# The last stage of a decoder: v in q's bank, the norm's root on GpSimd, copies swapped, one gelu from PSUM

## The chip, the cores and the metric

The kernel runs on one core of a Trainium2 chip. The metric is the device time in microseconds (us). Of the kernel before, 3 runs gave 2872.33 us in the median (2869.9 to 2873.28). In what follows PE is TensorE, DVE is VectorE, ACT is ScalarE, POOL is GpSimd and SP is SyncE, the queue that issues the DMAs.

## The reference

The program is a decoder of twelve stages over x of 4 batches, 256 tokens and width 128, all in float32. Only the last stage, `l3_ffn`, is touched. It is a small transformer of its own, six layers deep:

```
def ffn_layer(x, g, bln, W1, b1, W2, b2):
    mu = x.mean(-1, keepdims=True)
    var = ((x - mu) ** 2).mean(-1, keepdims=True)
    xn = (x - mu) / jnp.sqrt(var + 1e-05) * g + bln
    hg = xn @ W1 + b1
    a, gate = jnp.split(hg, 2, -1)
    return a * jax.nn.gelu(gate, approximate=False) @ W2 + b2
for i in range(DEPTH):                                    # 6
    x = attn_layer(shift_tokens(x), Wqkv[i], q_scale[i], k_scale[i], Wo[i]) + x
    x = ffn_layer(shift_tokens(x), ln_g[i], ln_b[i], W1[i], b1[i], W2[i], b2[i]) + x
```

`attn_layer` projects x to q, k and v (16 heads of 64), divides q and k by their norm in each head, scales and rotates them, and does a softmax attention of each block of 32 tokens to itself and the block before it. `shift_tokens` moves the upper half of the width by one token. The gates and ups of the feed-forward part are 341 wide.

## The kernel before

`l3_ffn` loads tables and weights, and calls `stream`, which is one software pipeline over the whole stage. A job is one layer of one batch: 6 x 4 = 24 jobs. A job has 8 pairs of heads, so 192 groups `g`, and 4 projection steps `u` (two halves of the heads by two blocks of 128 tokens), so 96 steps. Every engine walks the same list of ticks, one per group, and in each tick emits what is due there, in the order in which the code stands; constants say how many ticks a part of a job lies behind its first group. There is no scheduler: each engine runs its own list strictly in order, and semaphores hold it where data is missing.

In tick `s` each engine does this (names as in the code):

- PE: q's projection in even ticks (line 2077, into bank 0 of PSUM); k's (2086, bank 1) and v's (2091, bank 7) in odd ticks. Then the scores of group s (2101 adds the window mask, 2109), the turning of group s+1's q and k (2121, bank 3), the turning of group s-2's probabilities (2130), one part of a job's rest in bank 2, and the sums with v of group s-3 (2228, `heads`, the first half of bank 7).
- ACT: copies the heads of group s-4 out of bank 7 (signal `stored`), squares q or k, copies v out (`v_copied`), does the four exps of group s, copies the turned q and k of group s+1 (`net_qk_T`) if the group is even, and then the parts of a job's rest.
- DVE: the reciprocal of group s-1's sums (2407), the maximum of group s (2411), in some ticks the product for the last gate (2421), the two products of the rotation of q or k (2375 and 2381, signal `parted`), the copy of the turned probabilities, the copy of the turned q and k if the group is odd, the sums of squares (2447, even ticks), and the rest.
- POOL: multiplies group s-1's probabilities with the reciprocals (2337), in one tick of four the late half of a root for the head norms (8 steps, lines 1877 to 1880), scales group s+2 (2350), adds the rotation's two products (2329), in one tick of four the early half of the root (6 steps).

The rest of a job comes at fixed ticks, which repeat every 8 ticks, since a job has 8 groups. I number ticks by their remainder modulo 8. Tick 4 is OUT (2142, 32 matmuls). Tick 5 is LATE: PE shifts the tokens (2152 to 2154), DVE copies them to z, takes mean and variance (2464, 2467) and computes the inverse root with `root_of_variance`, eleven steps on a tile of 128x2, of which each waits for the one before (2393 to 2398), and the shift (2401). Tick 6 is SHIFT (2162). Tick 7 is ZT: ACT normalizes z with two ACTIVATEs (line 130) that wait for the root and stand ahead of that tick's exps, PE turns z (2171), ACT copies it out. Tick 0 is GATES: PE makes two thirds of the gates (2182), ACT adds the bias to each. Tick 1 is BOTH: PE makes the last third of the gates and of the ups (2190, 2191), ACT adds the bias to that third and does one gelu over all three (2309). Tick 2 is UPS: DVE first multiplies the last third (2421), then PE writes two thirds of the ups (2197), and DVE multiplies those (2479). Tick 3 is DOWN (2208).

ACT holds one table of functions at a time, and the program has an ACT_TABLE_LOAD ahead of the gelu and one ahead of the next exp.

Two rules set how v's matmul waits. v and `heads` lie in one bank, so v's matmul (2091) waits for `stored` of every group up to s-4, and the sums (2228) wait for `v_copied` of the last v. q's matmul waits for `parted` of the q before.

Of the kernel before, what the change touches and what calls it, by code (L numbers as in the profile page):

```python
# [16 lines left out]
I32 = mybir.dt.int32  # L17
# [8 lines left out]
QT = N // P  # L26
# [78 lines left out]
def decoder(nc, a, out):  # L105
    ctx = ExitStack()
    with ctx:
# [1690 lines left out]
        def l3_ffn():  # L1798
            sub = ExitStack()
            with sub:  # L1800
# [37 lines left out]
                made = signal("window_made", 4)  # L1838
                with nc.Block() as block:
                    @block.vector  # L1840
                    def _(dve):
                        nc.vector.tensor_copy(window16[:, :], window[:, :]).then_inc(made.sem, 1)
                        nc.vector.memset(gelu[:, :, :], 0.0).then_inc(made.sem, 1)
                        nc.vector.memset(by_batch(xnT[D // 2:D, :])[:, :, 0:1], 0.0).then_inc(made.sem, 1)
# [47 lines left out]
        def stream(p, GT, qkv_in, rows, weights, tables, heads_norm, ln, softmax, ffn):  # L1892
# [45 lines left out]
            LN_OPS = 11  # L1938
            ln_rooted, normed = signal("net_ln_rooted", LN_OPS * JOBS), signal("net_normed", 2 * JOBS)
            ln_shifted = signal("net_ln_shifted", JOBS)  # L1940
            z_turned, z_moved = signal("net_z_turned", JOBS), signal("net_z_moved", JOBS)
            gates_made, gates_moved = signal("net_gates_made", JOBS), signal("net_gates_moved", 3 * JOBS)
            both_made, gelued = signal("net_both_made", JOBS), signal("net_gelued", JOBS)
# [46 lines left out]
            def until_copied(eng, g):  # L1990

                if g >= 0:
                    e = ENG[g % 2]
                    eng.wait_ge(copied[e].sem, copied[e].at(0, g // 2 + 1))

            finished, sent = signal("net_finished", B), signal("net_sent", B, step=16)
            with ps("bank", [P, 8, BANK]) as bank, nc.Block() as block:
                qk_bank = (bank[:, 0, :], bank[:, 1, :])
                turn_bank, flip_bank = bank[:, 3, :], bank[:, 6, :]
                heads, v_bank = bank[:, 7, 0:N], bank[:, 7, :]  # L2000
# [55 lines left out]
                def _(pe):  # L2056
                    held, values_in = [], 0
# [6 lines left out]
                    for s in TICKS:  # L2064
                        u = at_tick(s, PROJ, 2, S)
                        if u is not None:
# [9 lines left out]
                            until(pe, parted, 2 * u - 1)  # L2076
                            nc.tensor.matmul(qk_bank[0], xnT[:, (QT * b + t) * P:(QT * b + t + 1) * P], w_qkv[:, half_cols(c)],  # L2077
                                             start=True, stop=True).then_inc(q_filled.sem, 1)
                        u = at_tick(s, PROJ + 1, 2, S)
                        if u is not None:  # L2080
# [12 lines left out]
                            values_in = u + 1  # L2093
# [81 lines left out]
                        if n is not None:  # L2175
# [9 lines left out]
                            held = [(gates_moved, 3 * n + 2)]  # L2185
# [28 lines left out]
                        if 0 <= g < G:  # L2214
# [8 lines left out]
                            until(pe, v_copied, values_in)  # L2223
# [9 lines left out]
                def _(act):  # L2233
# [7 lines left out]
                    for s in TICKS:  # L2241
# [37 lines left out]
                        if 0 <= g < G and g % 2 == 0:  # L2279
# [24 lines left out]
                        if n is not None:  # L2304
                            k = GT[2]
                            act.wait_ge(both_made.sem, both_made.at(0, n + 1))
                            affine("act", gelu[0:k, 2, :], spare[0:k, 0:N], 1.0, vec[0:k, 7:8]).then_inc(gates_moved.sem, 1)
                            act.wait_ge(gates_moved.sem, gates_moved.at(0, 3 * n + 3))
                            nc.scalar.activation(gelu[:, :, :], gelu[:, :, :], ACT.Gelu).then_inc(gelued.sem, 1)

                @block.gpsimd
                def _(pool):
# [19 lines left out]
                    for s in TICKS:  # L2332
# [33 lines left out]
                def _(dve):  # L2366
# [17 lines left out]
                    def root_of_variance(dve, n):  # L2384

                        lower, y, t = ln_temp[:, 0, :], ln_temp[:, 1, :], ln_temp[:, 2, :]
                        done = [LN_OPS * n]

                        def then(ins):
                            done[0] += 1  # L2390
                            ins.then_inc(ln_rooted.sem, 1)
                            dve.wait_ge(ln_rooted.sem, ln_rooted.at(0, done[0]))
                        then(nc.vector.tensor_scalar(lower, meanvar[:, 0:QT, 1], LN_EPS, -0.5, ALU.add, ALU.mult))
                        then(nc.vector.tensor_scalar(y.bitcast(I32), lower.bitcast(I32), -0.5, ROOT_MAGIC, ALU.mult, ALU.add))
                        for r in range(3):
# [235 lines left out]
```

## Time and profile before

| | us |
|---|---|
| median of 3 runs | 2872.33 |
| the profiled execution | 2870.53 |
| its span, first to last instruction | 2868.4 |
| last stage, first scores to last (L2101) | 1836.4 to 2824.8 |
| PE busy in the span | 2533.2 (88%) |
| DVE busy | 1777.3 (62%) |
| ACT busy | 1540.6 (54%) |
| POOL busy | 1363.8 (48%) |

The busy shares are over the whole span; the last stage is the 1050 us at its end. There the four engines are all busier, and the stage repeats itself every 8 ticks, so one period can be read closely and stands for the others. A row of the timeline gives the start, the length, the engine and line, and in brackets the idle time of that engine just before and what ended it. PEld is the load of weights that goes ahead of a matmul. PEclk is the clock that TensorE was granted, as a share of full speed.

### The profile page before, as it was taken

The numbers are of one execution on the slowest core, as the hardware profiler recorded it, in microseconds if no ns is written. First come the engines' busy times: TensorE is split into PE (matmuls) and PEld (weight loads), VectorE is DVE, ScalarE is ACT, GpSimd is POOL, SyncE is SP. The second block draws the span as 40 slices with busy tenths as digits, with TensorE's granted clock in tenths as the row PEclk, the third lists the DMA queues.
The fourth block names the chain that finished last, engine by engine and source line by source line (L and its number), as shares of the span: only waits on it lengthen the run. The fifth ranks groups of instructions, "written<-read, shape, count | busy, mean of one in ns | idle before, by whom it ended". The sixth has DMA issues, their size and how long they took to land. (4 is left out here: it accounts for less than half of the span.)

```text
span 2868.4 us, 57933 instructions
## 1 busy us (share of the span) xinstructions
PE 2533.2 (88%) x20585; PEld 1609.3 (56%) x20585; DVE 1777.3 (62%) x4074; ACT 1540.6 (54%) x4979; POOL 1363.8 (48%) x1981
## 2 busy tenths in 40 slices
PE   6999978988989979959289999689999999999996
PEld 3555545555645646646155555356666666666665
DVE  4556655545656755564645555677777777777773
ACT  1455534623746736623135555466667667666763
POOL 0344433401536623400004444587777777777772
PEclk8899997998989999989579999899999999999998
DMA  2000000000000010000010000200110101011000
GB/s 70 1 1 1 1 8 1 12 28 10 2 4 1 2 33 1 2 6 1 8 28 1 1 1 1 62 27 24 28 37 20 46 20 31 27 27 38 20 26 7
DMA packets 45711, 47.84 MB, mean 17 GB/s; under 512 B 11947, under 2 KB 31414, under 8 KB 45431
## 3 DMA queue, kind: packets, MB, share of 16 engines
q1 hardware_dynamic: 45430, 44.18, 5.6%
q8 instruction: 167, 2.74, 0.4%
q14 instruction: 114, 0.93, 0.1%
HBM read 31.05 MB, written 0.52 MB: 11 GB/s over the span
## 5 line engine op out<-in xcount | busy, mean ns | idle before, releaser
L1033 DVE TENSOR_REDUCE negmax<-scores 128x1 f32<-128x508 f32 (+4 forms) x512 | 212.6, 467 | 215.6 <-PE scores L918 184.4
L1013 POOL TENSOR_TENSOR l_xattn_probs<-l_xattn_probs,rowinv 128x512 f32<-128x512 f32 x128 | 130.3, 1039 | 421.1 <-DVE rowinv L1025 421.1
L2275 ACT ACTIVATE net_probs<-bank,net_negmax 128x96 f32<-128x96 f32 x768 | 251.7, 340 | 126.5 <-DVE net_negmax L2411 126.2
L1013 POOL TENSOR_TENSOR lora_probs<-lora_probs,rowinv 128x508 f32<-128x508 f32 (+1 forms) x256 | 149.5, 617 | 248.6 <-DVE rowinv L1025 248.6
L2329 POOL TENSOR_TENSOR net_rope<-net_rope,net_sin_parts 128x512 f32<-128x512 f32 x192 | 244.4, 1273 | 7.1 <-DVE net_sin_parts L2381 7.1
L2337 POOL TENSOR_TENSOR net_probs<-net_probs,net_inverse 128x384 f32<-128x384 f32 x192 | 158.7, 827 | 181.2 <-DVE net_inverse L2407 179.3
L2411 DVE TENSOR_REDUCE net_negmax<-bank 128x4 f32<-128x384 f32 x192 | 106.2, 553 | 196.0 <-PE bank L2109 195.3
L2350 POOL TENSOR_TENSOR net_rope<-net_rope,net_head_inv 128x512 f32<-128x512 f32 x192 | 201.2, 1048 | 7.5 <-POOL net_head_inv L1880 0.9
L124 DVE COPY turned<-flip 128x512 f32<-128x512 f32 (+3 forms) x280 | 163.2, 583 | 66.3 <-PE flip L945 52.3
L739 DVE TENSOR_REDUCE negmax<-scores 128x2 f32<-128x256 f32 (+2 forms) x192 | 157.8, 822 | 71.4 <-PE scores L647 42.0
L918 PE MATMUL scores<-kT,qM 64*128 64x512 f32 (+2 forms) x768 | 192.2, 577 | 6.0 <-ACT kT L122 2.5
L986 ACT ACTIVATE lora_probs<-scores,negmax 128x508 f32<-128x508 f32 (+1 forms) x256 | 117.8, 472 | 141.8 <-DVE negmax L1033 141.0
L122 ACT ACTIVATE turned<-flip 128x512 f32<-128x512 f32 (+3 forms) x280 | 143.5, 513 | 63.2 <-PE flip L661 53.1
L968 PE MATMUL heads<-turned,V 128*64 128x256 f32 (+1 forms) x1280 | 167.3, 383 | 2.0 <-ACT turned L122 1.4
L986 ACT ACTIVATE l_xattn_probs<-scores,negmax 128x512 f32<-128x512 f32 x128 | 86.9, 684 | 136.5 <-DVE negmax L1033 136.5
L2275 ACT ACTIVATION_READ_ACCUMULATOR net_probs<-bank,net_negmax 128x1 f32 x768 | 156.3, 204 | 0.0
L2121 PE MATMUL bank<-ident,net_rope 128*128 128x128 f32 x768 | 129.1, 292 | 26.5 <-POOL net_rope L2350 26.5
L2239 ACT ACTIVATE net_squares<-bank 128x512 f32<-128x512 f32 x192 | 115.2, 600 | 68.4 <-PE bank L2077 37.2
L724 POOL TENSOR_TENSOR cross_probs<-cross_probs,rowinv 128x1024 f32<-128x1024 f32 x64 | 119.8, 1893 | 66.3 <-DVE rowinv L734 66.3
L2091 PE MATMUL bank<-net_w_qkv,xnT 128*128 128x512 f32 x192 | 103.4, 620 | 40.7 <-ACT net_rope L122 40.7
L124 DVE COPY net_probs_turned<-bank 128x512 f32<-128x512 f32 x192 | 130.7, 681 | 13.4 <-PE bank L2130 13.3
L2375 DVE TENSOR_TENSOR net_rope<-bank,net_cos_table 128x512 f32<-128x512 f32 x192 | 130.9, 682 | 9.2 <-ACT net_squares L2239 9.1
(434 smaller groups left out, 6499.9 us busy)
## 6 DMA issues: line engine op xcount, KB each, us to landing
net_w_qkv<-in_L_ffn_Wqkv SPq DMA_DIRECT2D x12, 768.0 KB, 5.9
net_vals_between<-net_vals SPq DMA_DIRECT2D x48, 192.0 KB, 2.5
net_w_out<-in_L_ffn_Wo SPq DMA_DIRECT2D x6, 512.0 KB, 4.2
net_vals_between<-net_vals SPq DMA_DIRECT2D x48, 64.0 KB, 2.0
moe_w<-in_L_ffn_w13T SPq DMA_DIRECT2D x8, 256.0 KB, 2.7
net_w<-in_L_ffn_W SPq DMA_DIRECT2D x6, 341.0 KB
moe_w<-in_L_ffn_w2T SPq DMA_DIRECT2D x8, 128.0 KB, 2.3
ctx_tok<-in_ctx SPq DMA_DIRECT2D x1, 768.0 KB, 6.6
```

The costliest lines, as they stand in the source:

```text
L122: return nc.scalar.activation(dst, src, ACT.Copy, scale=scale)
L124: return nc.vector.tensor_copy(dst, src)
L739: nc.vector.tensor_reduce(negmax[:, c:c + 2], scores[:, 2 * half:2 * half + 2, 0:nk], AX.X, ALU.max, negate=True).then_inc(maxed.sem, 1)
L918: last = nc.tensor.matmul(scores[:, 2 * qt + h, 0:nk], qM[rows, 0, t * P:(t + 1) * P], kT[rows, k0:k0 + nk], start=True, stop=cross)
L968: last = nc.tensor.matmul(heads[rows, q0 * P:QT * P], V[:, v0 + j, rows], turned[:, 2 * p + h, c0:c0 + w], start=(j == 0), stop=(j == part ...
L986: last = nc.scalar.activation(pr[:, slot(g, qt, h), k0:k1], scores[:, 2 * qt + h, k0:k1], ACT.Exp, bias=negmax[:, u * tail + w:u * tail + ...
L1013: last = nc.gpsimd.tensor_tensor(own, own, rowinv[:, u * tail + w:u * tail + w + 1].to_broadcast([P, k1 - k0]), ALU.mult)
L1033: last = nc.vector.tensor_reduce(negmax[:, u * tail + w:u * tail + w + 1], scores[:, 2 * qt + h, k0:k1], AX.X, ALU.max, negate=True)
L2275: last = nc.scalar.activation(prob_blocks(g)[:, w, :], score_blocks(g)[:, w // 2, w % 2, :], ACT.Exp, bias=maxima[:, g % 4, w:w + 1], accu ...
L2329: nc.gpsimd.tensor_tensor(own, own, sin_parts[:, (2 * u + s) % 4, :], ALU.add).then_inc(added.sem, 1)
L2337: nc.gpsimd.tensor_tensor(prob_blocks(g), prob_blocks(g), part, ALU.mult).then_inc(shared.sem, 1)
L2350: nc.gpsimd.tensor_tensor(own, own, factor.to_broadcast([P, 4, 2, DH]), ALU.mult).then_inc(scaled.sem, 1)
```

## The change

Four things change, all in `stream`.

1. `v_bank` is bank 0, q's bank, instead of bank 7. v's matmul now waits for `parted` of the same step's q, and q's matmul waits for v's copy. The waits on `stored` ahead of v and on `v_copied` ahead of the sums go.
2. The norm's root leaves DVE. DVE writes variance plus epsilon and the negated mean (two steps), POOL raises the first to the power -0.5 and multiplies (two steps), one tick later. The exponents are a tile that DVE fills once.
3. Which engine copies the turned q and k is swapped: ACT now copies in even ticks, DVE in odd ticks.
4. The last third of the gates goes through the gelu straight from PSUM, with its bias; the gelu of the other two thirds follows. The DVE product of the last third waits only for the first of the two.

```
@@ -1990,14 +1990,14 @@
-                    e = ENG[g % 2]
+                    e = ENG[(g + 1) % 2]
...
-                heads, v_bank = bank[:, 7, 0:N], bank[:, 7, :]
+                heads, v_bank = bank[:, 7, 0:N], bank[:, 0, :]
@@ -2074,6 +2074,7 @@
                             until(pe, parted, 2 * u - 1)
+                            until(pe, v_copied, u)
...
-                            until(pe, stored, min(G, s - VALUES))
-                            until(pe, v_copied, u)
+                            until(pe, parted, 2 * u + 1)
...
                             until(pe, stored, g)
-                            until(pe, v_copied, values_in)
@@ -2304,9 +2302,9 @@
-                            affine("act", gelu[0:k, 2, :], spare[0:k, 0:N], 1.0, vec[0:k, 7:8]).then_inc(gates_moved.sem, 1)
-                            act.wait_ge(gates_moved.sem, gates_moved.at(0, 3 * n + 3))
-                            nc.scalar.activation(gelu[:, :, :], gelu[:, :, :], ACT.Gelu).then_inc(gelued.sem, 1)
+                            nc.scalar.activation(gelu[0:k, 2, :], spare[0:k, 0:N], ACT.Gelu, bias=vec[0:k, 7:8]).then_inc(gelued.sem, 1)
+                            act.wait_ge(gates_moved.sem, gates_moved.at(0, 2 * n + 2))
+                            nc.scalar.activation(gelu[:, 0:2, :], gelu[:, 0:2, :], ACT.Gelu).then_inc(gelued.sem, 1)
@@ -2358,6 +2356,14 @@
+                        n = at_tick(s, LATE + 1, PER, JOBS)
+                        if n is not None:
+                            pool.wait_ge(ln_ready.sem, ln_ready.at(0, 2 * n + 2))
+
+                            until(pool, normed, 2 * n)
+                            nc.gpsimd.tensor_tensor(ln_inv[:, :], ln_temp[:, 0, :], ln_temp[:, 2, :], ALU.pow).then_inc(ln_rooted.sem, 1)
+                            pool.wait_ge(ln_rooted.sem, ln_rooted.at(0, n + 1))
+                            nc.gpsimd.tensor_tensor(ln_shift[:, :], ln_temp[:, 1, :], ln_inv[:, :], ALU.mult).then_inc(ln_shifted.sem, 1)
@@ -2466,7 +2453,11 @@
-                            root_of_variance(dve, n)
+                            until(dve, ln_rooted, n)
+                            nc.vector.tensor_scalar(ln_temp[:, 0, :], meanvar[:, 0:QT, 1], LN_EPS, None, ALU.add).then_inc(ln_ready.sem, 1)
+
+                            until(dve, ln_shifted, n)
+                            nc.vector.tensor_scalar(ln_temp[:, 1, :], meanvar[:, 0:QT, 0], -1.0, None, ALU.mult).then_inc(ln_ready.sem, 1)
```

The lines of the new kernel carry other numbers: 2411 is 2398 there, 2350 is 2348, 2121 is 2120, 2091 is still 2091, 2309 is 2305 and 2307.

On DVE, from the copy of the turned probabilities in tick 5 to the first products of tick 6, this stands in a row before, the middle of the root left out:

```order
L124 COPY net_probs_turned<-bank 128x512 [waits net_summed,net_flipped]
L124 COPY z<-bank 128x2x64 [waits net_late_made]
L2464 BN_STATS stats<-z 128x6 [waits net_low_moved,net_late_moved]
L2464 BN_STATS stats<-z 128x6
L2467 BN_AGGR meanvar<-stats 128x2 [waits net_measured] x2
L2393 TENSOR_SCALAR net_ln_temp<-meanvar 128x2 [waits net_gathered]
...
L2398 SCALAR_TENSOR_TENSOR net_ln_inv<-net_ln_temp 128x2 [waits net_ln_rooted]
L2401 SCALAR_TENSOR_TENSOR net_ln_shift<-meanvar,net_ln_inv 128x2 [waits net_ln_rooted]
L2407 RECIPROCAL net_inverse<-net_sums 128x4 [waits net_exped]
L2411 TENSOR_REDUCE net_negmax<-bank 128x4 [waits net_scored]
```

and now:

```order
L124 COPY net_probs_turned<-bank 128x512 [waits net_summed,net_flipped]
L124 COPY net_qk_T<-bank 128x512 [waits net_scored,net_turned]
L124 COPY z<-bank 128x2x64 [waits net_late_made]
L2451 BN_STATS stats<-z 128x6 [waits net_low_moved,net_late_moved]
L2451 BN_STATS stats<-z 128x6
L2454 BN_AGGR meanvar<-stats 128x2 [waits net_measured] x2
L2457 TENSOR_SCALAR net_ln_temp<-meanvar 128x2 [waits net_ln_rooted,net_gathered]
L2460 TENSOR_SCALAR net_ln_temp<-meanvar 128x2 [waits net_ln_shifted]
L2394 RECIPROCAL net_inverse<-net_sums 128x4 [waits net_exped]
L2398 TENSOR_REDUCE net_negmax<-bank 128x4 [waits net_scored]
```

The eleven steps of the root and the one of the shift are two steps, and a copy of `net_qk_T` has come in ahead of the copy to z.

On POOL, from the end of the head norms' root in tick 6 to the first multiplication of tick 7, this stands in a row before:

```order
L1879 TENSOR_SCALAR net_head_temp<-net_head_temp 128x32 [waits net_norms_rooted]
L1880 TENSOR_TENSOR net_head_inv<-net_head_temp 128x32 [waits net_norms_rooted]
L2350 TENSOR_TENSOR net_rope<-net_rope,net_head_inv 128x4x128 [waits net_norms_rooted,net_parts_added]
L2329 TENSOR_TENSOR net_rope<-net_rope,net_sin_parts 128x512 [waits net_parted]
L2337 TENSOR_TENSOR net_probs<-net_probs,net_inverse 128x4x96 [waits net_inverted]
```

and now:

```order
L1880 TENSOR_SCALAR net_head_temp<-net_head_temp 128x32 [waits net_norms_rooted]
L1881 TENSOR_TENSOR net_head_inv<-net_head_temp 128x32 [waits net_norms_rooted]
L2348 TENSOR_TENSOR net_rope<-net_rope,net_head_inv 128x4x128 [waits net_norms_rooted,net_parts_added]
L2327 TENSOR_TENSOR net_rope<-net_rope,net_sin_parts 128x512 [waits net_parted]
L2364 TENSOR_TENSOR net_ln_inv<-net_ln_temp 128x2 [waits net_normed,net_ln_ready]
L2366 TENSOR_TENSOR net_ln_shift<-net_ln_temp,net_ln_inv 128x2 [waits net_ln_rooted]
L2335 TENSOR_TENSOR net_probs<-net_probs,net_inverse 128x4x96 [waits net_inverted]
```

The two steps of the norm stand behind the scaling and the addition of tick 6 and ahead of tick 7's probabilities.

On ACT, from the exps of tick 1 to the copy of the heads in tick 2, this stands in a row before:

```order
L2275 ACTIVATE net_probs,net_sums<-bank,net_negmax 128x96 [waits net_flipped,net_maxed]
L2275 ACTIVATE net_probs,net_sums<-bank,net_negmax 128x96 x3
L122 ACTIVATE net_qk_T<-bank 128x512 [waits net_scored,net_turned]
L130 ACTIVATE net_gelu<-bank,net_layer_cols 85x256 [waits net_both_made]
L2309 ACT_TABLE_LOAD
L2309 ACTIVATE net_gelu<-net_gelu 128x768 [waits net_gates_moved]
L122 ACTIVATE net_rope<-bank 128x2x128 [waits net_summed]
```

and now:

```order
L2273 ACTIVATE net_probs,net_sums<-bank,net_negmax 128x96 [waits net_flipped,net_maxed]
L2273 ACTIVATE net_probs,net_sums<-bank,net_negmax 128x96 x3
L2305 ACT_TABLE_LOAD
L2305 ACTIVATE net_gelu<-bank,net_layer_cols 85x256 [waits net_both_made]
L2307 ACTIVATE net_gelu<-net_gelu 128x512 [waits net_gates_moved]
L122 ACTIVATE net_rope<-bank 128x2x128 [waits net_summed]
```

The copy of `net_qk_T` and the bias step are gone from between the exps and the table load, and the gelu is two instructions.

## Rows read from the trace of the kernel before

**Rows 1.** Waits, 1840 to 2850: engine line <- releaser: us total, times, longest.

```profile
PE bank L2091 <- ACT net_rope L122: 40.7, 43, 1.5
...
PE bank L2121 <- POOL net_rope L2350: 23.4, 27, 3.2
```

**Rows 2.** Windows of the last stage: length, busy (xinstructions), PEclk, DMA share, GB/s.

```profile
1996.26:2039.49 43.23, 40.15 (x411) 27.55 (x411) 31.93 (x71) 28.89 (x100) 34.61 (x58) 0.96 0.09 26
...
2334.04:2375.71 41.67, 38.59 (x411) 26.20 (x410) 31.84 (x71) 28.44 (x100) 33.03 (x56) 1.00 0.10 27
...
2334.04:2349.47 15.43, 14.49 (x143) 8.85 (x142) 11.69 (x21) 12.88 (x40) 14.21 (x27) 1.00 0.01 2
...
2349.47:2361.68 12.21, 12.21 (x132) 9.59 (x132) 7.86 (x16) 5.85 (x22) 9.16 (x11) 1.00 0.16 41
...
2361.68:2375.71 14.03, 11.89 (x139) 7.75 (x138) 12.29 (x35) 9.71 (x38) 9.66 (x21) 1.00 0.15 43
```

**Rows 3.** Timeline (start us, us, engine line op): first and last regular period starts, ticks 0.

```profile
1912.92 0.28 PE L2101 MATMUL bank<-net_window,ident 64*64 64x192 bf16 x4
...
2753.78 0.28 PE L2101 MATMUL bank<-net_window,ident 64*64 64x192 bf16 x4
```

**Rows 4.** Timeline, ticks 5 to 7: DVE's root, and who waits.

```profile
2322.94 0.28 DVE L124 COPY z<-bank 128x128 f32<-128x128 f32 x1
...
2323.99 0.17 DVE L2393 TENSOR_SCALAR net_ln_temp<-meanvar 128x2 f32<-128x2 f32 x1
...
2326.23 0.17 DVE L2407 RECIPROCAL net_inverse<-net_sums 128x4 f32<-128x4 f32 x1
...
2326.48 0.83 POOL L2337 TENSOR_TENSOR net_probs<-net_probs,net_inverse 128x384 f32<-128x384 f32 x1 [3.14 <-DVE net_inverse L2407]
...
2328.85 1.12 PE L2091 MATMUL bank<-net_w_qkv,xnT 128*128 128x512 f32 x2 [1.50 <-ACT net_rope L122]
...
2330.04 1.05 POOL L2350 TENSOR_TENSOR net_rope<-net_rope,net_head_inv 128x512 f32<-128x512 f32 x1
...
2332.28 0.83 POOL L2337 TENSOR_TENSOR net_probs<-net_probs,net_inverse 128x384 f32<-128x384 f32 x1
```

**Rows 5.** Timeline, tick 7: z, its turning, and the next tick 0.

```profile
2330.51 0.87 ACT L130 ACTIVATE z<-z,net_ln_shift,net_ln_inv 128x128 f32<-128x128 f32 x2
...
2331.97 0.25 PEld L2171 LDWEIGHTS bank<-ident,z 128*128 128x128 f32 x2
...
2334.04 0.28 PE L2101 MATMUL bank<-net_window,ident 64*64 64x192 bf16 x4
```

**Rows 6.** Timeline, ticks 1 and 2: the gates.

```profile
2341.99 0.48 ACT L130 ACTIVATE net_gelu<-bank,net_layer_cols 85x256 f32<-85x256 f32 x1
...
2343.78 0.84 ACT L2309 ACTIVATE net_gelu<-net_gelu 128x768 f32<-128x768 f32 x1
...
2343.72 0.56 DVE L2411 TENSOR_REDUCE net_negmax<-bank 128x4 f32<-128x384 f32 x1 [1.64 <-PE bank L2109]
...
2344.73 0.48 DVE L2421 SCALAR_TENSOR_TENSOR net_acts<-bank,net_layer_cols,net_gelu 85x256 f32<-85x256 f32 x1 [0.46 <-ACT net_gelu L2309]
...
2345.26 0.73 PEld L2197 LDWEIGHTS bank<-net_znT,net_w 128*128 128x128 f32 x4 [0.81 <-DVE net_acts L2421]
```

**Rows 7.** Chain of waits: start us, us, what; a v matmul without a wait.

```profile
2319.22 0.86 PE bank L2091 x2
```

**Rows 8.** Groups by line and form, POOL: xcount | busy us, mean ns | idle.

```profile
L1013 POOL TENSOR_TENSOR lora_probs<-lora_probs,rowinv 128x4 f32<-128x4 f32 x128 | 25.8, 201 | 0.0
...
L1878 POOL TENSOR_TENSOR net_head_temp<-net_head_temp 128x32 f32<-128x32 f32 x144 | 36.3, 252 | 11.3
```

**Rows 9.** Window over two stands of PE, columns as in Rows 2.

```profile
2284.27:2288.09 3.82, 1.69 (x23) 0.71 (x22) 3.73 (x8) 3.09 (x12) 3.10 (x10) 0.94 0.00 0
```

**Rows 10.** Chain of waits at the end of the span.

```profile
2831.19 0.47 ACT net_gelu L130
...
2833.93 0.49 DVE net_acts L2421
```

More of the change, by code:

```diff
@@ L1837, in l3_ffn @@
                 norm(x, NT, D, xin, loads=wanted, begin=first, clear=probs[:, :, :])
-                made = signal("window_made", 4)
+                made = signal("window_made", 5)
                 with nc.Block() as block:
@@ L1843, in _ @@
                         nc.vector.memset(gelu[:, :, :], 0.0).then_inc(made.sem, 1)
+                        nc.vector.memset(ln_temp[:, 2, :], -0.5).then_inc(made.sem, 1)
                         nc.vector.memset(by_batch(xnT[D // 2:D, :])[:, :, 0:1], 0.0).then_inc(made.sem, 1)
@@ L2056, in _ @@
                 def _(pe):
-                    held, values_in = [], 0
+                    held = []
                     def take_spare():
@@ L2184, in _ @@
                             last.then_inc(gates_made.sem, 1)
-                            held = [(gates_moved, 3 * n + 2)]
+                            held = [(gates_moved, 2 * n + 2)]
                         n = at_tick(s, BOTH, PER, JOBS)
@@ L2278, in _ @@
                         g = s + TURN
-                        if 0 <= g < G and g % 2 == 0:
+                        if 0 <= g < G and g % 2 == 1:
                             act.wait_ge(turned.sem, turned.at(0, g + 1))
@@ L2382, in part @@
                                                 ALU.mult).then_inc(parted.sem, 1)
[L2384 to L2395, printed above, removed]
-                            then(nc.vector.tensor_tensor(t, y, y, ALU.mult))
-                            then(nc.vector.tensor_tensor(t, t, lower, ALU.mult))
-                            then(nc.vector.scalar_tensor_tensor(y if r < 2 else ln_inv[:, :], t, 1.5, y, ALU.add, ALU.mult))
-                        assert done[0] == LN_OPS * (n + 1)
-                        nc.vector.scalar_tensor_tensor(ln_shift[:, :], meanvar[:, 0:QT, 0], -1.0, ln_inv[:, :], ALU.mult, ALU.mult).then_inc(ln_shifted.sem, 1)
                     for s in TICKS:
@@ L2419, in _ @@
                             dve.wait_ge(both_made.sem, both_made.at(0, n + 1))
-                            dve.wait_ge(gelued.sem, gelued.at(0, n + 1))
+                            dve.wait_ge(gelued.sem, gelued.at(0, 2 * n + 1))
                             nc.vector.scalar_tensor_tensor(acts[0:k, 2, :], spare[0:k, N:2 * N], vec[0:k, 4:5], gelu[0:k, 2, :], ALU.add,
@@ L2435, in _ @@
                         g = s + TURN
-                        if 0 <= g < G and g % 2 == 1:
+                        if 0 <= g < G and g % 2 == 0:
                             dve.wait_ge(turned.sem, turned.at(0, g + 1))
@@ L2477, in _ @@
                             dve.wait_ge(ups_made.sem, ups_made.at(0, n + 1))
+                            dve.wait_ge(gelued.sem, gelued.at(0, 2 * n + 2))
                             for j in range(2):
```

8 lines of the change are left out of this document (3 added, 5 removed).

## The prediction

> **What bounds the kernel now.** I read the page's busy shares and slices first: the last stage is the last 1050 us, and there PE is busy nine tenths. Then the waits of that stretch, then the timeline of one period, and windows over its parts.
>
> The stage repeats itself. From the first to the last regular tick 0 there are 20 periods in 2753.78 - 1912.92 = 840.86 us [rows 3]. A period without a fall of the clock takes 41.67 us, one with a fall 43.23, at a mean granted clock of 0.96 [rows 2]. So the excess over 20 x 41.67 = 833.4 is 7.5 us, five falls of about 1.5 us each.
>
> PE works 38.59 of the 41.67 us [rows 2]. By parts: ticks 0 to 2 take 15.43 us with 14.49 busy, ticks 3 and 4 take 12.21 and are full, ticks 5 to 7 take 14.03 with 11.89 busy. So PE bounds the stage, and 3.1 us in a period are stands. Nothing in this change shortens PE's work, so no more than these can go, and what matters is which wait ends last at each stand. The long ones: v's matmul waits for the copy of the heads, 40.7 us in 43 times, and the turning of q and k waits for POOL's scaling, 23.4 us in 27 times [rows 1]. In tick 6 v's wait is 1.50 us [rows 4]; 22 of these are 33 us, which leaves 7.7 us for the 21 others, 0.37 each. The latter lie in tick 2. There PE also waits for DVE's product of the last third, which ACT's gelu holds up (0.46 us) [rows 6].
>
> **Ticks 0 to 2: the gelu, the copies and v's bank.** ACT runs, without a pause, the copy of q and k, the bias step (0.48), the table load and the gelu (0.84, ended at 2344.62), and only then does DVE start its product at 2344.73 [rows 6]. The change takes the copy and the bias step out of this row and lets DVE go after the first gelu, of 85x256. Even if that takes as long as the whole one, 0.84, it ends more than 0.4 us sooner than now by the bias step alone. What is late next is DVE itself: its maximum runs from 2343.72 to 2344.28 [rows 6]. So the product starts at 2344.28 and not 2344.73, and PE's ups 0.45 us sooner. Then v: it waits no more for the heads (0.37), and it waits for the product of q from the tick before, which DVE finishes well ahead. A v matmul that follows k's directly takes 0.86 in the chain [rows 7], against 1.12 after a wait [rows 4]: 0.26 more. Together 0.45 + 0.37 + 0.26 = 1.08 us a period. Bounds: 0.82 if the 0.26 is only the shape of the record, 1.3 if DVE's maximum overlaps its product's start. Ticks 3 and 4 are full of PE [rows 2], and the swapped copy costs neither engine's queue anything there that PE would wait for; I cost the swap at nothing. Without that cover it costs one copy, some 0.6 us.
>
> **Ticks 5 to 7: the root.** v's bank takes away 1.50 us of stand in tick 6, and 0.26 of length. But that is not what ends this stretch. The chain runs through DVE's root to the reciprocal, to POOL's probabilities, through eight steps of the head norms' root to the scaling (2330.04), and PE's turning in tick 7 waits for that [rows 4]. The root takes from 2323.99 to 2326.23, 2.24 us. It goes; two steps of 0.17 come, 0.34, and one copy of q and k now stands ahead of the copy to z, about 0.6. So the reciprocal, and all of POOL behind it, comes 1.3 us sooner (1.2 to 1.5).
>
> The new part is a wait. ACT's two steps on z stand ahead of tick 7's exps in its queue, and PE's turning of z stands ahead of the sums and the next q in PE's. Before, the root was long done (z at 2330.51 [rows 5]). Now POOL gives it after the scaling and the addition. In POOL's row that place is where now the next probabilities start, 2332.28 [rows 4], so 2330.98 after the shift of 1.3. Behind the power, of length p, come the multiplication and the handing over, about 0.25 (a small product on POOL takes 0.20 [rows 8]). Then ACT's two steps, 0.87, and 0.05 to PE: PE's turning of z starts at 2332.15 + p. Before, it started at 2331.97 [rows 5], and from there to tick 0 is PE's own work, which stays. So this stretch grows by 0.18 + p. Queued behind the wait are ACT's exps of tick 7 and PE's sums and q.
>
> **The power's price.** The trace has no power. Below, p can hardly be less than POOL's product of 128x4, 0.20. Above, I take the eleven steps of the root as eleven POOL steps of 0.25 in one instruction, 2.8 [rows 8]. A step on 128x32 costs only 0.05 more than one on 128x4, so most of a small step is its fixed part, which is paid once here. I therefore stay near the low row and take p = 0.3.
>
> The Trainium skill says against this change that GpSimd is the wrong engine for elementwise arithmetic, about twice as slow as VectorE (GPSIMD Engine Reference, When to use GPSIMD). By that, a step of DVE's 0.17 would be 0.34 here, and the sum by it would be about 1 us worse over the stage; it gives no price for a power, and the trace only half agrees, since 0.20 and 0.25 for small tiles are less than twice 0.17.
>
> Without falls of the clock a period changes by -1.08 + 0.18 + 0.3 = -0.60 us, times 22 is -13.2.
>
> **The clock.** Before each fall PE had two stands close together: in 3.82 us it was busy 1.69, and the clock was at its lower level, 1.2 of 2.4 GHz, at the end [rows 9]. Five of 22 such places fell. In the changed kernel the stand in tick 6 is gone and v's matmul ends at 2328.85 - 1.50 + 0.86 = 2328.2. The turning of q and k could start half a microsecond later, but comes only at 2331.1 - 1.3 = 2329.8: a stand of 1.1. Then z: PE is ready at 2331.97 - 1.3 = 2330.67 and goes on at 2332.15 + p: a stand of 1.5 + p. That is 2.9 us of standing in some 3.8, where it was 2.1. So falls get more frequent. Between 5 and 22 I take 10, five more, 7.5 us.
>
> The Trainium skill has a rule for this: short idle times between groups of matmuls, if frequent enough, make the clock swing between its levels, without one long gap (TensorE: Matmul & The Clock Gate, A second HAM failure mode: psum-queue depth-cycling). The trace agrees, by the 0.94 in its row. Read strictly, it says that every tick 7 falls; that is the first rival.
>
> **The end.** In the last jobs all is exposed. DVE's product at 2833.93 would start right after a gelu that itself starts where the bias step did, 2831.19 [rows 10], for 0.5: 2.2 us sooner, since the table can be loaded before. In the last job the root's 2.24 becomes 0.34 + 0.3 + 0.4, a gain of 1.2, and the gelu about 0.8. Together -4.2.
>
> **The sum.** -13.2 + 7.5 - 4.2 = -9.9 us against the profiled execution's 2870.5: 2860.6. The median of the runs is 1.8 us above the profiled one, so 2862.4 on its scale.
>
> **Rivals.**
> The clock falls in nearly every tick 7 (slower). Place: PE's two stands there. For it: 2.9 us of standing against 2.1 before, and more if p is larger. Against: in 17 of 22 places the clock held before, and a shift of the stands may meet that. Price: 17 more falls, 25.5 us. At p = 0.5: -8.8 + 25.5 - 4.2 = +12.5, so 2885. It decides from 18 falls on at p = 0.5, from 21 at p = 0.3.
> The power is dear, 1.2 us or more (slower). For it: nothing here bounds it. At p = 1.8, with falls in every period: 22 x 0.9 + 25.5 - 3 = +42, so 2915.
> The gain and the falls cancel: p = 0.4 and 15 falls give -11.0 + 15 - 4.2 = 0, so 2872.
> The stands in tick 7 lie so that the clock falls no more often than now, or never: -17 to -25, so 2847 to 2855. For it: a stand is gone from tick 6.
>
> **How the numbers follow.** 0.2% is 5.7 us, about what a measurement of this kernel can tell from no change. The forecast, 2862 (2856 to 2867), 0.34; no more falls, 0.15; no change, 0.11; falls everywhere, 0.30; a dear power, 0.10. Faster 0.49, same 0.11, slower 0.40. The range leaves out the dearest powers and reaches from 2844 to 2912.
>
> **What would show it.** Ticks 0 to 2 at about 14.35 us instead of 15.43, with no wait of v for ACT. The product of the last third 0.45 us sooner. In tick 7 PE waits twice, for POOL's scaling and for ACT's z, and ACT waits for POOL's multiplication ahead of z. The power's row gives p at once; over 0.9 it alone undoes the gain. I am wrong if z is not waited for, or if the stage's granted clock falls in most tick 7s.

## The result and the profile after

The changed kernel is slower: 2882.49 us (median of 20 runs, 2863.61 to 2891.53) against 2866.95 of the kernel before (20 runs, 2855.31 to 2873.28). The ratio is 1.0065, with the interval 1.0052 to 1.0079. The forecast was 2862. The profiled execution took 2882.05 us, with a span of 2880.3; before these were 2870.53 and 2868.4. One of the six runs of the kernel with filled stands, below, took 10371.84 us: it is in that kernel's median and not in its ratio, and without it the median is 2834.61.

The waits of the last stage, 1840 to 2860 us (engine, line, what released it: total us, times, longest), where [rows 1] stood:

```profile
ACT z L130 <- POOL net_ln_shift L2366: 66.1, 22, 3.2
...
PE bank L2170 <- ACT z L130: 44.1, 22, 2.0
...
PE bank L2120 <- POOL net_rope L2348: 28.2, 25, 4.3
...
PEld bank L2196 <- DVE net_acts L2408: 7.3, 23, 1.1
```

PE's wait of v for ACT's copy is gone. In its place PE waits for ACT's z, 22 times, and ACT waits for POOL's product behind the power, 66.1 us in all. The wait for the scaling stays.

Windows of the kernel after, columns as in [rows 2]: one period, then the parts of the next one (ticks 0 to 2, 3 and 4, 5 to 7), two single microseconds of a tick 7, and the regular stretch of the stage:

```profile
2425.84:2469.86 44.02, 41.07 (x412) 28.25 (x411) 30.23 (x61) 28.53 (x99) 32.43 (x55) 0.93 0.16 49
2469.86:2484.11 14.25, 14.22 (x143) 8.93 (x143) 11.11 (x20) 12.69 (x40) 10.30 (x22) 1.00 0.01 2
2484.11:2496.31 12.20, 12.20 (x131) 9.59 (x130) 7.67 (x16) 6.10 (x23) 8.94 (x10) 1.00 0.09 24
2496.31:2511.51 15.20, 12.27 (x139) 7.82 (x138) 11.36 (x26) 9.52 (x37) 12.26 (x25) 0.97 0.07 19
...
2420.80:2421.80 1.00, 0.00 (x0) 0.00 (x0) 0.68 (x2) 0.57 (x2) 0.92 (x3) 1.00 0.03 8
...
2424.80:2425.80 1.00, 1.00 (x2) 0.00 (x0) 0.00 (x0) 0.00 (x0) 1.00 (x2) 0.50 0.00 0
1900.00:2740.00 840.00, 781.82 (x7933) 533.73 (x7930) 582.91 (x1178) 552.90 (x1922) 638.35 (x1059) 0.94 0.10 29
```

The same stretch of the kernel before:

```profile
1900.00:2740.00 840.00, 778.35 (x8191) 529.79 (x8193) 636.69 (x1420) 569.97 (x1979) 637.95 (x1053) 0.99 0.11 30
```

Ticks 0 to 2 take 14.25 us instead of 15.43, and PE is busy in all but 0.03 of them. Ticks 3 and 4 are unchanged. Ticks 5 to 7 take 15.20 instead of 14.03, in a period that ends with a short fall of the clock and takes 41.65 in all; a period that spends more time at the lower clock, as the first row's (0.93), takes 44.02. In tick 7 PE stands (from 2420.80 to 2421.80 it does nothing), and soon after its clock is at the lower of its two levels (0.50 in the row from 2424.80). Over 840 us the mean granted clock is 0.94, before it was 0.99. That is the number that matters most, and the page's 0.923 against 0.931 for the whole span hides it, because all other stages are in there too.

The first and the last regular tick 0 of the kernel after, answering [rows 3]:

```profile
1905.52 0.37 PE L2100 MATMUL bank<-net_window,ident 64*64 64x192 bf16 x4
...
2770.92 0.37 PE L2100 MATMUL bank<-net_window,ident 64*64 64x192 bf16 x4
```

So 20 periods take 865.40 us, 43.27 each, where it was 42.04. The two spans compare like this:

| stretch | before | after | difference |
|---|---|---|---|
| up to the last stage (PE's L1177) | 1799.22 | 1790.14 | -9.08 |
| from there to the first regular tick 0 | 113.70 | 115.38 | +1.68 |
| 20 periods | 840.86 | 865.40 | +24.54 |
| from the last regular tick 0 on | 114.62 | 109.38 | -5.24 |

The first line is code that the change doesn't touch: the two executions differ by that much there. The loss lies in the periods; 1.68 more come ahead of them, and the end gives 5.24 back.

Ticks 5 to 7 of one period after, the timeline behind [rows 4, 5]:

```profile
2412.93 0.28 DVE L124 COPY z<-bank 128x128 f32<-128x128 f32 x1
...
2413.98 0.17 DVE L2457 TENSOR_SCALAR net_ln_temp<-meanvar 128x2 f32<-128x2 f32 x1
2414.06 0.16 DVE L2460 TENSOR_SCALAR net_ln_temp<-meanvar 128x2 f32<-128x2 f32 x1
2414.13 0.17 DVE L2394 RECIPROCAL net_inverse<-net_sums 128x4 f32<-128x4 f32 x1
...
2414.38 0.83 POOL L2335 TENSOR_TENSOR net_probs<-net_probs,net_inverse 128x384 f32<-128x384 f32 x1 [1.64 <-DVE net_inverse L2394]
...
2416.58 1.02 PE L2091 MATMUL bank<-net_w_qkv,xnT 128*128 128x512 f32 x2
...
2417.95 1.05 POOL L2348 TENSOR_TENSOR net_rope<-net_rope,net_head_inv 128x512 f32<-128x512 f32 x1
...
2419.06 0.66 PE L2120 MATMUL bank<-ident,net_rope 128*128 128x128 f32 x4 [0.92 <-POOL net_rope L2348]
...
2420.20 0.72 POOL L2364 TENSOR_TENSOR net_ln_inv<-net_ln_temp 128x2 f32<-128x2 f32 x1
...
2420.99 0.20 POOL L2366 TENSOR_TENSOR net_ln_shift<-net_ln_temp,net_ln_inv 128x2 f32<-128x2 f32 x1
2421.15 0.83 POOL L2335 TENSOR_TENSOR net_probs<-net_probs,net_inverse 128x384 f32<-128x384 f32 x1
2421.23 0.88 ACT L130 ACTIVATE z<-z,net_ln_shift,net_ln_inv 128x128 f32<-128x128 f32 x2 [2.99 <-POOL net_ln_shift L2366]
...
2422.16 0.69 PE L2170 MATMUL bank<-ident,z 128*128 128x128 f32 x2 [2.01 <-ACT z L130]
...
2425.84 0.37 PE L2100 MATMUL bank<-net_window,ident 64*64 64x192 bf16 x4
```

DVE's root is two steps, 2413.98 and 2414.06, and the reciprocal follows at 2414.13. POOL's probabilities, the scaling (2417.95) and PE's turning of it all come sooner, and v's matmul (2416.58) waits for nothing. Then POOL adds, takes the power (0.72 us) and the product (0.20). ACT starts z 0.04 us after that. PE, ready since 2420.15, goes on at 2422.16. From there its instructions are longer (0.69 for z's turning).

The gates of the kernel after, answering [rows 6], and the chain at the end, answering [rows 10]:

```profile
2478.76 0.47 ACT L2305 ACTIVATE net_gelu<-bank,net_layer_cols 85x256 f32<-85x256 f32 x1
...
2479.53 0.56 DVE L2398 TENSOR_REDUCE net_negmax<-bank 128x4 f32<-128x384 f32 x1 [1.05 <-PE bank L2108]
...
2480.01 0.47 DVE L2408 SCALAR_TENSOR_TENSOR net_acts<-bank,net_layer_cols,net_gelu 85x256 f32<-85x256 f32 x1
...
2480.53 0.73 PEld L2196 LDWEIGHTS bank<-net_znT,net_w 128*128 128x128 f32 x4 [0.27 <-DVE net_acts L2408]
```

```profile
2849.42 0.48 ACT net_gelu L2305
...
2849.99 0.49 DVE net_acts L2408
```

DVE's product (2480.01) now follows its own maximum with no wait for ACT, and the wait of PE's weight load (PEld) for it fell from 0.81 to 0.27. In the last job the bias step, the table load and the second gelu no longer lie between: the product starts 0.57 us behind the start of the gelu, where it was 2.74 behind the bias step. The instructions that [rows 8] had to stand in for, by groups of POOL (xcount | busy us, mean ns):

```profile
L2364 POOL TENSOR_TENSOR net_ln_inv<-net_ln_temp 128x2 f32<-128x2 f32 x23 | 16.6, 723 | 0.0
...
L2366 POOL TENSOR_TENSOR net_ln_shift<-net_ln_temp,net_ln_inv 128x2 f32<-128x2 f32 x23 | 4.5, 196 | 1.8
```

### The profile page after: what moved, and what is told of

Read it like the earlier page. It is cut to its first block and busy times, and to the rows that moved or that the text cites. A ratio compares the mean times of both kernels' runs of the same rounds, so it can differ in the third digit from the quotient of the medians.

```text
span 2880.3 us, 57759 instructions
## 1 busy us (share of the span) xinstructions
PE 2550.6 (89%) x20585; PEld 1624.6 (56%) x20585; DVE 1737.7 (60%) x3835; ACT 1538.3 (53%) x4979; POOL 1387.4 (48%) x2029
## 3 DMA queue, kind: packets, MB, share of 16 engines
q8 instruction: 167, 2.74, 0.4%
## 5 line engine op out<-in xcount | busy, mean ns | idle before, releaser
L2226 PE MATMUL bank<-net_probs_turned,net_vals 128*64 128x128 f32 (+1 forms) x1536 | 136.3, 270 | 0.0
```

What stands on the lines that cost most here:

```text
L2226: last = nc.tensor.matmul(heads[rows_of(h), w0 * QB:w1_ * QB], own[:, c * D + h * DH:c * D + (h + 1) * DH], given[:, h, r0:r1, a, :], star ...
```

## The experiments

All times are medians, and ratios are against the kernel before on the same chip, with their intervals. "Undisturbed" is a period in which the clock doesn't fall; falls are counted in the profile from 1900 to 2745 us, some 20 periods. In some kernels one period in four is up to 0.8 us longer in ticks 3 and 4 without a fall; these are left out of the undisturbed ones. Before has 5 falls and after 20, one in each period. Twelve of these kept the clock at 1.2 GHz for 3.4 us, like all five of before, and eight for 6.8.

A count is of one execution, and it varies: the mean granted clock of the 20 runs of the kernel after lies between 0.919 and 0.933. Their times follow it, from 2863.61 us at 0.933 to 2891.53 at 0.920. The eight runs of the kernel before with 0.933 took 2866.44 to 2871.12 us, so at an equal clock the kernel after isn't the slower one. Small differences of a count, as between 4 and 5, say nothing.

The theory after the result: the steps work as forecast, but with a power of 0.72 us PE's two stands in tick 7 make the clock fall every time. The rival: the clock only accompanies a wait that costs as much by itself.

**Filling the stands.** Five matmuls whose results nobody uses are put where PE stands in tick 7, two ahead of the wait for the scaling and three ahead of z. The waits for the two banks that they write move ahead of them.

```diff
+                            until_copied(pe, g - 1)
+                            if at_tick(s, ZT, PER, JOBS) is not None:
+                                for r in range(2):
+                                    nc.tensor.matmul(turn_bank[:, 0:N], ident[:, :], late[:, :, :], start=True, stop=True)
                             pe.wait_ge(scaled.sem, scaled.at(0, g + 1))
-                            until_copied(pe, g - 1)
...
+                            take_spare()
+                            for r in range(3):
+                                nc.tensor.matmul(spare[:, 0:N], ident[:, :], late[:, :, :], start=True, stop=True)
                             pe.wait_ge(normed.sem, normed.at(0, 2 * n + 2))
-                            take_spare()
```

> The changed kernel with five extra matmuls of 128x256 in each tick 7, two ahead of the turning of q and k and three ahead of the turning of z, where TensorE stands; nobody reads what they write. Clock theory (the stands of tick 7 make the clock fall in every period, and that is the loss): no fall in tick 7, tick 7 about 6.7 us, tick 0 4.94, a period 41.3 us instead of 43.27, ratio to before 0.991 to 0.994. Wait theory (the later z is the loss by itself, the clock comes along): at least as slow as the changed kernel, ratio 1.006 or more.

Measured: 2838.29, ratio 0.9919 (0.9888 to 0.9951). Its windows (a period, its tick 7, the regular stretch) and PE in that tick 7:

```profile
2356.33:2397.56 41.23, 40.49 (x422) 28.06 (x422) 30.13 (x61) 28.28 (x99) 32.58 (x56) 1.00 0.10 28
2390.91:2397.56 6.65, 5.94 (x56) 4.01 (x56) 3.95 (x9) 3.58 (x14) 6.40 (x9) 1.00 0.16 42
1900.00:2740.00 840.00, 824.54 (x8556) 570.81 (x8556) 612.05 (x1240) 579.28 (x2025) 670.27 (x1115) 1.00 0.11 30
```

```profile
2391.44 1.13 PE L2119 MATMUL bank<-net_late,ident 128*128 128x256 f32 x4
...
2393.36 1.46 PE L2172 MATMUL bank<-net_late,ident 128*128 128x256 f32 x6
2395.53 0.44 PE L2175 MATMUL bank<-ident,z 128*128 128x128 f32 x2 [0.71 <-ACT z L130]
```

No fall in the periods, and each of them takes 41.23 us. PE has more to do than in the kernel after and is 2.0 us a period faster. z's turning starts 4.62 us after tick 7's start, in the kernel after 4.63 (2422.16 - 2417.53): the added matmuls delay nothing, and the waits are the same. So the difference, 43.27 - 41.23, is the clock alone. It also shows what the change is worth without it: 41.23 against 41.67.

**A cheap step in the power's place.** The power becomes a product of two constants. This leaves the root of the norm out.

```diff
-                            nc.gpsimd.tensor_tensor(ln_inv[:, :], ln_temp[:, 0, :], ln_temp[:, 2, :], ALU.pow).then_inc(ln_rooted.sem, 1)
+                            nc.gpsimd.tensor_tensor(ln_inv[:, :], ln_temp[:, 2, :], ln_temp[:, 2, :], ALU.mult).then_inc(ln_rooted.sem, 1)
```

> The changed kernel with a product of two constants in place of the power, so the norm's root is not computed and the time alone counts; the same waits, a length of 0.20 instead of 0.72 us. Clock theory: z comes 0.5 us sooner, the stands shrink to 2.7 us in sum, the clock falls in some ticks 7 only and never for two stretches: a period about 41 to 42, ratio to before 0.990 to 1.000. Wait theory: 22 times 0.5 us, 11 us less than the changed kernel, ratio 1.002 to 1.003.

Measured: 2848.7, ratio 0.9954 (0.9937 to 0.9972). The step takes 0.20:

```profile
L2364 POOL TENSOR_TENSOR net_ln_inv<-net_ln_temp 128x2 f32<-128x2 f32 x24 | 4.7, 195 | 15.2 <-DVE net_ln_temp L2460 15.2
```

Tick 7 undisturbed is 6.10 us where it is 6.65 in the kernel with filled stands: the half microsecond of the step comes off in full. The ratio lies where the clock theory put it, and far from the other's 1.002 to 1.003. There are 11 falls, but five of them last 6.8 us, where I had expected none to last so long. PE's waits, 1900 to 2740:

```profile
PE bank L2170 <- ACT z L130: 29.5, 20, 1.5
PE bank L2120 <- POOL net_rope L2348: 18.1, 20, 0.9
```

The stands are 2.4 us in sum, less than the 2.9 for which the prediction took 10 falls. Its 20 periods take 835.57 us, 21.8 more than 20 undisturbed ones of 40.69; ten falls at the forecast's 1.5 are 15.

**The root back on DVE**, the rest of the change kept (DVE's eleven steps as before, no power):

```diff
+            LN_OPS = 11
...
-                            nc.gpsimd.tensor_tensor(ln_inv[:, :], ln_temp[:, 0, :], ln_temp[:, 2, :], ALU.pow).then_inc(ln_rooted.sem, 1)
...
+                            root_of_variance(dve, n)
```

> The changed kernel with the root back on VectorE as before; v's bank, the swapped copies and the gelu stay. Clock theory: the root and the copy ahead of it hold up the reciprocal 0.6 us longer than before, TensorE stands about 3 us in one piece in tick 7 and the clock falls there in most periods: a period about 42.6, ratio 1.000 to 1.005. Theory that the root's move is the whole loss: the other three parts gain their 1.1 us a period, ratio 0.990.

Measured: 2854.5, ratio 0.997 (0.9947 to 0.9993). Both expectations missed. Undisturbed periods take 41.10 us, and the clock fell only 4 times. PE in its ticks 6 and 7:

```profile
2447.13 1.13 PE L2091 MATMUL bank<-net_w_qkv,xnT 128*128 128x512 f32 x2 [1.35 <-DVE net_sin_parts L2379]
...
2450.20 0.66 PE L2120 MATMUL bank<-ident,net_rope 128*128 128x128 f32 x4 [1.40 <-POOL net_rope L2348]
```

The stands are 1.35 us in tick 6 and 1.40 in tick 7, 2.75 in all within the 4.42 us from 2445.78 to 2450.20, with 1.67 of work between them, and z isn't waited for. In the kernel after they are 0.92 and 2.01, 2.93 in all within 4.02 us, with 1.09 of work between. So nearly as much standing, less crowded, gave 4 falls and not 20. My expectation had gone by the amount of standing and was too coarse.

**The root alone** (before, with only the power and its product on POOL; the diff is the last one reversed):

> The kernel before with only the root moved to GpSimd. Clock theory: the stretch of ticks 5 to 7 is 0.2 us longer by its waits, but its stands lie in tick 7 and the clock falls nearly always: a period near 43.4, ratio 1.008 to 1.011. Wait theory: 22 times 0.2 us, ratio 1.001 to 1.002.

Measured: 2871.36, ratio 1.0023 (1.0002 to 1.0044). PE's waits, 1900 to 2740:

```profile
PE bank L2171 <- ACT z L130: 39.9, 20, 2.0
...
PE bank L2091 <- ACT net_rope L122: 7.5, 20, 0.4
```

PE waits 2.0 us for z here as well. An undisturbed period is 41.79, 0.12 longer than before, and the clock fell 10 times, where the clock theory had wanted more. The ratio is near the 1.001 to 1.002 of the other theory, and by itself wouldn't decide between them. The trace does: 20 periods take 850.15 us, 9.3 more than before, of which the longer undisturbed period is 2.4. In tick 7 PE's other stand is short here, 0.3 for the scaling, where the kernel after has 0.92; the 0.4 for v is in tick 2.

**The other three parts alone**, each put into the kernel before. The bank of v:

> The kernel before with only v's bank changed. The wait of v in tick 6 should turn into waits for VectorE's copy and for GpSimd's scaling, with the stretch of ticks 5 to 7 at 14.03 as before; ticks 0 to 2 gain about 0.4 to 0.6 us. Clock theory: the stands add up to 2.5 us where they were 2.1, so some more falls take back a part: ratio 0.995 to 1.000. If the bank's wait were the bound: 1.5 us more a period, ratio 0.980.

The gelu from PSUM:

> The kernel before with only the last gate's gelu taken straight from PSUM. The product of the last third starts about 0.45 us sooner, when VectorE's maximum ends; ticks 0 to 2 gain 0.3 to 0.5 us, ticks 5 to 7 stay at 14.03, the end of the span gains 2 to 4 us; the clock falls as often as before: ratio 0.995 to 0.997. If the saved step was hidden: ratio 0.999 to 1.001.

The swapped copies (`g % 2` to `(g + 1) % 2` and the two parities):

> The kernel before with only the copies of the turned rows swapped. If the copy in tick 5 stands in the chain: ticks 5 to 7 are 0.6 us longer, 14.6, ticks 0 to 2 are 0.4 to 0.5 us shorter because ScalarE has one copy less ahead of the gelu, more stands in ticks 6 and 7 and some more falls of the clock: ratio 1.000 to 1.006. If the swap evens out the engines as such: 0.994 to 0.997.

| part alone | us | ratio | undisturbed period | falls |
|---|---|---|---|---|
| v's bank | 2849.95 | 0.9939 (0.9921 to 0.9957) | 41.06 | 2 |
| gelu | 2850.28 | 0.9975 (0.9961 to 0.9989) | 41.46 | 4 |
| swap | 2896.69 | 1.0131 (1.0108 to 1.0154) | 42.58 | 16 |
| root (above) | 2871.36 | 1.0023 (1.0002 to 1.0044) | 41.79 | 10 |

v's bank takes 0.63 from ticks 0 to 2, the 0.37 + 0.26 of the prediction, and leaves ticks 5 to 7 at 14.05. Of the stand of tick 6, 0.76 stays, now as a wait for DVE's product of q, and the rest comes back in tick 7 as a wait for the scaling of 1.26 instead of 0.63. The clock falls no more often all the same (median granted clock 0.9375, before on that chip 0.933), which I had expected the other way round, and the ratio is below the range I gave. The gelu takes 0.21 from ticks 0 to 2, half of what I gave it. The swap was costed at nothing and is the dearest part, beyond even the 1.000 to 1.006 expected of it here. Its timeline at the end of tick 5 and in tick 6:

```profile
2417.62 0.68 DVE L124 COPY net_qk_T<-bank 128x512 f32<-128x512 f32 x1
...
2418.22 0.28 DVE L124 COPY z<-bank 128x128 f32<-128x128 f32 x1
...
2424.61 1.12 PE L2091 MATMUL bank<-net_w_qkv,xnT 128*128 128x512 f32 x2 [2.58 <-ACT net_rope L122]
```

DVE copies q and k just ahead of z, which puts z and all that follows the root 0.6 us later. v, still waiting for the heads, waits 2.58 us instead of 1.50, and ticks 5 to 7 take 14.63 instead of 14.03. Ticks 0 to 2, where I had expected a gain, take 15.74 instead of 15.43: PE's wait for the last third's product nearly goes, but v's for the heads in tick 2 is 0.82 instead of 0.37. Together the four ratios multiply to 1.0067, close to the whole change's 1.0065. That is a coincidence: undoing the swap in the kernel after gives -1.1%, undoing the root -0.9%, which doesn't add up with what they cost alone.

**The swap undone** in the kernel after:

```diff
-                    e = ENG[(g + 1) % 2]
+                    e = ENG[g % 2]
...
-                        if 0 <= g < G and g % 2 == 1:
+                        if 0 <= g < G and g % 2 == 0:
...
-                        if 0 <= g < G and g % 2 == 0:
+                        if 0 <= g < G and g % 2 == 1:
```

> The changed kernel with the copies of the turned rows on the engines of before. If the swap is what holds up VectorE in tick 5: the reciprocal, GpSimd's scaling and z all 0.6 us sooner, tick 7 about 6.1 without a fall, the clock still falls there in most periods, a period about 42.2, ratio 0.998 to 1.002. If the swap is a gain by itself: slower than the changed kernel, ratio above 1.0065, with ticks 0 to 2 longer than 14.3 us.

Measured: 2857.22, ratio 0.9957 (0.9937 to 0.9977), somewhat better than expected. Tick 7 is 6.03, 0.62 shorter; an undisturbed period 40.67; 12 falls, five of them of 6.8 us. Ticks 0 to 2 are 14.25, as in the kernel after.

**The power earlier.** POOL takes the power and the product ahead of tick 6's addition instead of behind it.

```diff
+                        n = at_tick(s, LATE + 1, PER, JOBS)
+                        if n is not None:
+                            pool.wait_ge(ln_ready.sem, ln_ready.at(0, 2 * n + 2))
...
                         u = at_tick(s, PROJ + 2, 2, S)
                         if u is not None:
                             add_parts(u, 1)
```

> The changed kernel with the power and its product one place earlier in GpSimd's queue, ahead of tick 6's addition instead of behind it. Theory of place and clock: z comes 1.23 us sooner, TensorE stands 1.0 and about 1.0 us in tick 7, no more than before the change, so the clock falls seldom: tick 7 about 5.5, a period about 40.1 without falls and 40.4 with, ratio to before 0.984 to 0.988. Theory that a root on GpSimd costs its length and its falls wherever it stands: 22 times 1.23 less than the changed kernel, ratio 0.996 to 0.998.

Measured: 2825.46, ratio 0.9851 (0.9812 to 0.9891). Tick 7 is 5.42 as expected, since z no longer waits behind an addition of 1.28 us. PE's waits, 1900 to 2740:

```profile
PE bank L2120 <- POOL net_rope L2348: 22.5, 25, 1.0
PE bank L2170 <- ACT z L130: 16.2, 21, 0.8
```

There are 9 falls, in an execution that was the slowest of the four runs (2836.88): more than in the kernel before, with less standing.

**Both**, the power earlier and the swap undone:

> Both: the power ahead of the addition, and the copies on the engines of before. Theory of place and clock: the stands of tick 7 are 0.4 and 1.0 us, the clock does not fall there, tick 7 about 4.9, a period about 39.5, ratio 0.978 to 0.982. The other theory: ratio 0.990 to 0.995.

Measured: 2803.34 (4 runs, 2801.72 to 2814.78), ratio 0.9796 (0.9755 to 0.9836). This beats both kernels. A period, and the regular stretch; then PE's waits in it:

```profile
2338.68:2378.15 39.47, 38.34 (x412) 26.38 (x411) 30.04 (x61) 28.18 (x100) 32.51 (x56) 1.00 0.11 29
1900.00:2740.00 840.00, 811.71 (x8702) 558.96 (x8704) 636.74 (x1291) 597.92 (x2108) 696.69 (x1155) 1.00 0.11 31
```

```profile
PE bank L2170 <- ACT z L130: 17.0, 22, 0.8
PE bank L2120 <- POOL net_rope L2348: 10.4, 25, 1.0
```

PE still waits for z, but for 0.8 us, not 2.0. The clock never falls in this stretch of the profiled execution. An undisturbed period is 39.47 us with PE busy 38.34 of it.

**Stands and falls together.** PE's stands in ticks 6 and 7 of each kernel (in the order of time, from the timelines), its work between them, and the falls of its profiled execution:

| kernel | stands, us | work between, us | falls (of 6.8 us) |
|---|---|---|---|
| before | 1.50, 0.63 | 1.66 | 5 (0) |
| gelu alone | 1.50, 0.63 | 1.66 | 4 (0) |
| v's bank alone | 0.76, 1.26 | 1.80 | 2 (0) |
| swap alone | 2.58 | | 16 (1) |
| root alone | 0.31, 2.00 | 1.09 | 10 (0) |
| after | 0.92, 2.01 | 1.09 | 20 (8) |
| filled | 0.71 | | 0 |
| cheap step | 0.91, 1.48 | 1.09 | 11 (5) |
| root back | 1.35, 1.40 | 1.67 | 4 (1) |
| swap undone | 0.31, 2.00 | 1.09 | 12 (5) |
| power earlier | 0.92, 0.77 | 1.09 | 9 (0) |
| both | 0.33, 0.77 | 1.09 | 0 |

Neither the sum of the stands nor how close they lie gives the count: 1.69 us of standing led to 9 falls and 2.75 to 4, and the same stands to 10 short falls in one kernel and to 12, five of them long, in another. That the stands make the clock fall is shown by filling them; what sets how often is open.

## Why the prediction was wrong

**Right: ticks 0 to 2.** Forecast -1.08 us, measured 14.25 against 15.43, -1.18. By its parts: v gives 0.63 (forecast 0.63), the gelu alone only 0.21. In the kernel after DVE's product starts 10.15 us behind tick 0 and before 10.69, the 0.45 of the forecast and a little more. Alone, the gelu wins less because of v: PE's wait of 0.57 for the product goes, but its next wait, v's for the heads in tick 2, grows from 0.37 to 0.71. With v in q's bank that one is gone as well, and 0.57 + 0.37 + 0.26 is 1.20. The swap has no part in it, as these ticks take 14.25 with it undone, too.

**Right: the path through ticks 5 to 7.** The prediction's formula, +0.18 + p, gives +0.90 with the measured power. The undisturbed stretch (3.83 + 4.29 + 6.65 = 14.77 us, the last from the kernel with filled stands, whose waits are the same) is +0.74, since POOL's scaling came 1.5 us sooner and not 1.3. PE waits for z, and ACT for POOL, where the prediction put these waits.

**Wrong in size: the power.** p was 0.72 us; the bounds were 0.20 and 2.8, and I took 0.3, by the argument that most of a small step is a fixed part. The fixed part doesn't bound the operation itself. By this term alone a period still gains 0.44 us, so the kernel would be faster, as the one with filled stands shows. The Trainium skill's rule that GpSimd is about twice as slow as VectorE in elementwise work on two inputs (GPSIMD Engine Reference, When to use GPSIMD) would give 0.34 for it, an estimate from DVE's 0.17. The measured row is twice that, so the rule is no price for a power.

**Wrong, and decisive: the falls of the clock.** The step that failed is "Between 5 and 22 I take 10". There were 20 in 20 periods. The count was a choice between bounds, and nothing in it was worked out from the stands. It didn't fail for want of them: the prediction had 2.9 us of standing and 2.93 were measured, by luck, as the longer power and the earlier scaling nearly cancel. The power's length does matter for the count: with 0.20 in its place there are 11 falls. But five of those are long and they cost 21.8 us, so the clock's term was too small for a cheap power as well. That a fall can last twice as long, as eight of the 20 did, no term foresaw. Over the 20 periods:

| term | forecast | measured |
|---|---|---|
| steps | -0.60 x 20 = -12.0 | (41.23 - 41.67) x 20 = -8.8 |
| clock, on top of before's 7.5 | +7.5 | 20 x (43.27 - 41.23) - 7.5 = +33.3 |
| behind the periods | -4.2 | -5.2 |

The first rival (the clock falls in nearly every tick 7) is what happened. It gave 2885, and the profiled run took 2882.05; that the two are so near is partly luck, since the stages ahead of the last one, which the change doesn't touch, took 9.08 us less, and the falls cost more than the 25.5 us of the rival. The Trainium skill's rule for it, that short idle times between groups of matmuls can, if frequent enough, make the clock swing (TensorE: Matmul & The Clock Gate, A second HAM failure mode: psum-queue depth-cycling), agrees with the trace: the stands were 0.92 and 2.01 us (the windows and the timeline above), and the clock fell in each period. It names no count, so that every tick 7 must fall was the prediction's own reading of it, and it doesn't tell the kernel with 10 falls from the one with 20.

**Wrong: the swap at nothing.** I looked for its cover in ticks 3 and 4, where PE is full. The place that counts is tick 5, where the copy stands ahead of z on DVE. I did count that 0.6 there, inside the net 1.3 by which the reciprocal moves up, but didn't price the swap as an edit that could be left out. Undone, tick 7 shortens by 0.62, from 6.65 to 6.03.

## What to carry to other kernels

Where an engine's clock depends on how busy it is, look at the stands that lie close together, not only at the path, and count the falls in a trace, since no sum of stands gave their number here: a change that shortened the undisturbed period by 1% made the kernel 0.65% slower, and matmuls that compute nothing, in the same stands, gave 1.5% back. When a step moves to another engine, its place in that engine's queue is as important as its price: ahead of one addition instead of behind it, the same power left the kernel 2% faster. And of a change with several parts, time each alone and look at each part's queue, the one that seemed free first.

## What the runs showed of the hardware

- A power of 128x2 on POOL takes 0.72 us (0.69 to 0.73 in the 24 of the kernel after), a product of the same size 0.20.
- A fall of TensorE's clock to 1.2 GHz lasted 3.4 us in before, and 3.4 or 6.8 in the kernel after (12 and 8 times) and in four others, e.g. with the cheap step (6 and 5 times). The 95.6 us at the lower level that the regular stretch held cost 40.8 us, 0.43 us for each. Why some last twice as long is open.
- Stands of 1.35 and 1.40 us with 1.67 us of work between them led to 4 falls in 20 periods, and 0.92 and 2.01 us with 1.09 between them to 20. Filled with matmuls, the latter led to none. Stands of 0.92 and 0.77 us with 1.09 between them led to 9, so more standing isn't always more falls.
- The time of the kernel before moves by itself with the clock: between two executions, 2850.35 and 2872.25 us, the mean granted clock was 0.941 and 0.931.
